# Layer 1's product scan keeps its last value in a 449th column of shifted PSUM banks, and one copy of twelve columns per band replaces twelve copies of one

## The reference

```
x_dbl = einsum('kd,bdl->bkl', x_proj_w, xs)
dts, Bs, Cs = (x_dbl[:, :R], x_dbl[:, R:R + N], x_dbl[:, R + N:])
delta = softplus(einsum('dr,brl->bdl', dt_w, dts) + dt_b)
log_dA = maximum(delta * A, LOG_EPS)
P = exp(cumsum(log_dA))
dB_u = delta * Bs * xs
hs = P * cumsum(dB_u / maximum(P, EPS))
y = einsum('bdnl,bnl->bdl', hs, Cs) + xs * Ds
```

## Time and profile before

| | us |
|---|---|
| median of three runs | 4020.88 |
| lowest and highest | 4011.57, 4022.5 |
| the profiled execution, its own time | 4020.36 |
| its span | 4018.6 |
| mean granted TensorE clock, share of full | 0.928 |
| start of the first product scan (group 0) | 1956.5 |
| start of the last group | 3765.1 |

### The profile page before, as it was taken

The page is one execution under the profiler, slowest core; times in us unless marked ns, Lnnn a source line. Parts: engine busy times, 40 slices in busy tenths (PEclk is TensorE's granted clock), DMA queues, the critical chain, the costliest instruction groups (busy, mean ns, idle before and its releaser), DMA issues. The chain is left out here.

```text
span 4018.6 us, 72697 instructions
## 1 busy us (share of the span) xinstructions
PE 3650.8 (91%) x22358; PEld 2646.6 (66%) x22358; DVE 3106.0 (77%) x4416; ACT 2571.1 (64%) x4292; POOL 2575.8 (64%) x2672
## 2 busy tenths in 40 slices
PE   6999999999999999997899998998989989899776
PEld 6888787979787887877565564664646646466322
DVE  3675758475756667570499998999989989989999
ACT  1463728172735546274688787787778878777754
POOL 0352717162634536270488888888979889888988
PEclk9999999999999999998799898998989989989877
DMA  7546473747465554428565564655546646465222
GB/s 225 170 138 204 104 250 95 251 102 234 109 200 149 164 181 125 149 76 181 130 177 143 162 170 124 172 152 147 164 127 181 169 125 173 129 168 158 86 75 60
DMA packets 383746, 612.84 MB, mean 153 GB/s; under 512 B 199967, under 2 KB 324152, under 8 KB 383048
## 3 DMA queue, kind: packets, MB, share of 16 engines
q1 hardware_dynamic: 383336, 607.74, 53.5%
HBM read 527.35 MB, written 80.28 MB: 151 GB/s over the span
## 5 line engine op out<-in xcount | busy, mean ns | idle before, releaser
L321 POOL TENSOR_TENSOR h_low<-act_h,h_high 128x448 fp32r<-128x448 f32 x448 | 598.0, 1354 | 724.1 <-ACT h_high L520 723.9
L515 ACT ACTIVATE act_h<-ps_up,b 128x448 f32<-128x448 f32 x672 | 408.7, 635 | 728.5 <-PE ps_up L633 728.2
L1348 PE MATMUL ps_y<-h,ident 128*128 128x448 f32 x1344 | 727.1, 629 | 144.3 <-POOL h L1036 113.1
L1036 POOL TENSOR_TENSOR h<-h,c_rows 128x448 f32<-128x448 f32 x672 | 763.7, 1136 | 51.2 <-DVE h L1126 5.7
L1023 POOL TENSOR_TENSOR u<-dxs,b_rows 128x448 f32<-128x448 f32 x672 | 764.5, 1138 | 27.9 <-DVE ps_q L1115 16.8
L1099 DVE TENSOR_TENSOR_SCAN ps_q<-d_a,q_last,ps_q 128x448 f32<-128x448 f32 x576 | 659.5, 1145 | 0.0
L1126 DVE TENSOR_TENSOR_SCAN h<-d_a,h_last,ps_q 128x448 f32<-128x448 f32 x576 | 645.3, 1120 | 0.0
L1300 PEld LDWEIGHTS ps_front<-win,taps 120*112 120x112 f32 x4608 | 540.5, 188 | 149.2 <-issue 147.2
L606 PE MATMUL ps_stage<-win,taps 124*112 124x112 f32 x6144 | 608.3, 261 | 2.7 <-DVE w_low L368 2.7
L606 PEld LDWEIGHTS ps_stage<-win,taps 124*112 124x112 f32 x6144 | 608.1, 178 | 3.2 <-DVE w_low L368 2.8
L1205 ACT ACTIVATE d_a<-delta,log_eps,a_neg 128x448 f32<-128x448 f32 x672 | 503.3, 750 | 114.0 <-DVE h L1126 58.5
(11 more groups left out here) (81 smaller groups left out, 6212.6 us busy)
## 6 DMA issues: line engine op xcount, KB each, us to landing
taps<-in_t_dram SPq DMA_DIRECT2D x192, 896.0 KB, 5.0
taps<-in_t_dram SPq DMA_DIRECT2D x192, 672.0 KB, 4.7
b_rows<-bc_dram SPq DMA_DIRECT2D x224, 224.0 KB, 3.0
c_rows<-bc_dram SPq DMA_DIRECT2D x224, 224.0 KB, 3.1
xres<-in_x_dram SPq DMA_DIRECT2D x224, 168.0 KB, 2.5
x_dram<-x1o SPq DMA_DIRECT2D x224, 168.0 KB, 2.0
x1pad<-x_dram SPq DMA_DIRECT2D x96, 392.0 KB, 6.0
out_dram<-y SPq DMA_DIRECT2D x168, 224.0 KB, 2.6
```

The costliest lines, as they stand in the source:

```text
L321: nc.gpsimd.tensor_tensor(h_low[u % 2][:, t, :], act_h[u % 2][:, t, :], h_high[u % 2][:, t, :], ALU.subtract).then_inc(h_low_ready[t], 1)
L515: nc.scalar.activation(act_h[u % 2][:, t, :], ps_up[t][:, 0:BT], ACT.Gelu, bias=b1[:, t:t + 1]).then_inc(gelu_done, 1)
L1036: nc.gpsimd.tensor_tensor(h[s % H_SLOTS][:, :], h[s % H_SLOTS][:, :], c_rows[n][:, :], ALU.mult).then_inc(hc_done, 1)
L1348: nc.tensor.matmul(total, ident[:, :], h[s % H_SLOTS][:, :], start=False, stop=(n == N - 1)).then_inc(y_added, 1)
```

## The change

- `ps_q` becomes one tensor of two banks of 512 columns. A step of number j in its band uses bank j % 2 and starts in column 5 - j // 2, so that each use of a bank begins one column lower than the last one.
- The product scan runs over 449 columns. Column 448 of every d_a buffer is set to 1.0 once, by seven GpSimd memsets at the layer's start, and ScalarE writes only the first 448. The 449th value of the scan is then the last value of q once more; it lies one column beyond what the next step in that bank writes, and so stays.
- After the twelfth step's scan, one copy takes the six kept columns of both banks (128x12) into `q_last`; twelve copies of one column are gone. The gates no longer wait for `q_kept`; only the first product scan of a band does.

```diff
-        d_a = [sb(f"d_a{i}", [128, BT]) for i in range(DA_SLOTS)]
+        d_a = [sb(f"d_a{i}", [128, BT + 1]) for i in range(DA_SLOTS)]
-        ps_q = [pb(f"ps_q{i}") for i in range(2)]
+        ps_q = ctx.enter_context(nc.psum_tensor("ps_q", [128, 2, BANK], F32))
-        no_q = ps_q[0][:, BT:BT + 1]
+        no_q = ps_q[:, 0, BANK - 1:BANK]
+        PAIRS = STEPS // 2
+        def q_start(s):
+            return PAIRS - 1 - s % STEPS // 2
+        def q_bank(s, cols=BT):
+            return ps_q[:, s % 2, q_start(s):q_start(s) + cols]
+        def q_carry(s):
+            k = s % 2 * PAIRS + q_start(s)
+            return q_last[:, k:k + 1]
+            for k in range(DA_SLOTS):
+                nc.gpsimd.memset(d_a[k][:, BT:BT + 1], 1.0).then_inc(prepared, 1)
 def scan_q(g, s):
-                if s > 1:
-                    dve.wait_ge(q_kept, g * KEPT + min(s - 1, KEPT))
-                first = q_first[:, 0:1] if b == 0 else q_last[:, j:j + 1]
-                nc.vector.tensor_tensor_scan(ps_q[s % 2][:, 0:BT], d_a[s % DA_SLOTS][:, :],
-                                             no_q.broadcast_to([128, BT]), first,
+                if b > 0 and j == 0:
+                    dve.wait_ge(q_kept, g * (BANDS - 1) + b)
+                nc.vector.tensor_tensor_scan(q_bank(s, BT + 1), d_a[s % DA_SLOTS][:, :],
+                                             no_q.broadcast_to([128, BT + 1]), q_first[:, 0:1] if b == 0 else q_carry(s),
                                              ALU.mult, ALU.add).then_inc(q_done, 1)
-            def keep_q(g, s):
-                b, j = s // STEPS, s % STEPS
-                if b + 1 < BANDS:
-                    dve.wait_ge(q_done, g * S + s + 1)
-                    nc.vector.tensor_copy(q_last[:, j:j + 1], ps_q[s % 2][:, BT - 1:BT]).then_inc(q_kept, 1)
+            def keep_q(g, b):
+                dve.wait_ge(q_done, g * S + (b + 1) * STEPS)
+                nc.vector.tensor_copy(q_last[:, :].rearrange("p (k j) -> p k j", k=2),
+                                      ps_q[:, :, BT:BT + PAIRS]).then_inc(q_kept, 1)
 def gate(g, s):
-                if b + 1 < BANDS:
-                    dve.wait_ge(q_kept, g * KEPT + s + 1)
 def group(g, more):
-                    keep_q(g, s)
+                    if j == STEPS - 1 and b + 1 < BANDS:
+                        keep_q(g, b)
```

More of the change, by code:

```diff
@@ L800, in layer1 @@
         BORDERS = 4
-        PREPARED = 4 + TILES + 1
+        PREPARED = 4 + TILES + 1 + DA_SLOTS
         S = BANDS * STEPS
@@ L1095, in scan_q @@
                 dve.wait_ge(h_done, g * S + max(s, 1))
-                if s > 1:
-                    dve.wait_ge(q_kept, g * KEPT + min(s - 1, KEPT))
-                first = q_first[:, 0:1] if b == 0 else q_last[:, j:j + 1]
-                nc.vector.tensor_tensor_scan(ps_q[s % 2][:, 0:BT], d_a[s % DA_SLOTS][:, :],
-                                             no_q.broadcast_to([128, BT]), first,
-                                             ALU.mult, ALU.add).then_inc(q_done, 1)
-            def keep_q(g, s):
-                b, j = s // STEPS, s % STEPS
-                if b + 1 < BANDS:
-                    dve.wait_ge(q_done, g * S + s + 1)
-                    nc.vector.tensor_copy(q_last[:, j:j + 1], ps_q[s % 2][:, BT - 1:BT]).then_inc(q_kept, 1)
+                if b > 0 and j == 0:
+                    dve.wait_ge(q_kept, g * (BANDS - 1) + b)
+                nc.vector.tensor_tensor_scan(q_bank(s, BT + 1), d_a[s % DA_SLOTS][:, :],
+                                             no_q.broadcast_to([128, BT + 1]), q_first[:, 0:1] if b == 0 else q_carry(s),
+                                             ALU.mult, ALU.add).then_inc(q_done, 1)
+            def keep_q(g, b):
+                dve.wait_ge(q_done, g * S + (b + 1) * STEPS)
+                nc.vector.tensor_copy(q_last[:, :].rearrange("p (k j) -> p k j", k=2),
+                                      ps_q[:, :, BT:BT + PAIRS]).then_inc(q_kept, 1)
             def gate(g, s):
-                b = s // STEPS
                 dve.wait_ge(q_done, g * S + s + 1)
-                if b + 1 < BANDS:
-                    dve.wait_ge(q_kept, g * KEPT + s + 1)
                 dve.wait_ge(u_done, g * S + s + 1)
-                nc.vector.scalar_tensor_tensor(ps_q[s % 2][:, 0:BT], ps_q[s % 2][:, 0:BT], 1.0, u[s % U_SLOTS][:, :],
+                nc.vector.scalar_tensor_tensor(q_bank(s), q_bank(s), 1.0, u[s % U_SLOTS][:, :],
                                                ALU.min, ALU.mult).then_inc(gated, 1)
@@ L1125, in scan_h @@
                     first = h_last[:, j:j + 1]
-                nc.vector.tensor_tensor_scan(h[s % H_SLOTS][:, :], d_a[s % DA_SLOTS][:, :], ps_q[s % 2][:, 0:BT], first,
+                nc.vector.tensor_tensor_scan(h[s % H_SLOTS][:, :], d_a[s % DA_SLOTS][:, 0:BT], q_bank(s), first,
                                              ALU.mult, ALU.add).then_inc(h_done, 1)
@@ L1204, in clip_a @@
                     act.wait_ge(h_done, g * S + s - DA_SLOTS + 2)
-                nc.scalar.activation(d_a[s % DA_SLOTS][:, :], delta[:, t, :], ACT.Relu, bias=log_eps[:, 0:1],
+                nc.scalar.activation(d_a[s % DA_SLOTS][:, 0:BT], delta[:, t, :], ACT.Relu, bias=log_eps[:, 0:1],
                                      scale=a_neg[:, t, n:n + 1]).then_inc(clipped, 1)
@@ L1210, in exp_a @@
                 act.wait_ge(clipped, g * S + s + 1)
-                nc.scalar.activation(d_a[s % DA_SLOTS][:, :], d_a[s % DA_SLOTS][:, :], ACT.Exp,
+                nc.scalar.activation(d_a[s % DA_SLOTS][:, 0:BT], d_a[s % DA_SLOTS][:, 0:BT], ACT.Exp,
                                      bias=LOG_EPS).then_inc(d_a_ready, 1)
```

## The result

The changed kernel took 3986.5 us, the median of six runs (3978.3 to 4003.1), beside 4021.7 us for the kernel before: a ratio of 0.9916, with a 95% interval of 0.9890 to 0.9941. In a later comparison (run 11) it took 3972.7 us against 4029.2, a ratio of 0.9858 (0.9836 to 0.9880). Forecast were 3960 us, 61 less; it gained 35 and 57 us. The first gain is nearly rival B's 31 us, the second nearly the forecast's.

What follows compares the result with a forecast made beforehand. VectorE was taken to set undisturbed bands, with other engines close behind. Looped groups 45.5 us plus last group 15.5 us gave 61 us off 4020.4, rounded to 3960 us; own range 3940 to 3978, stated range 3925 to 3998.

Steps and rivals of the forecast that it cites:

- rival B: Looped groups: TensorE's chain holds them, waits move to before sum_delta; 31 us gained, 3989 us (3975 to 4005); chance 0.22.
- What bounds the kernel now: Layer 1: VectorE, busy 34.78 of 35.20 us, sets the length of an undisturbed band; other engines close behind.
- What a copy costs: VectorE's steps, bands 0 to 5: 0.19 us per copy in looped groups, 0.25 in the last; 114 us in all.
- What is added: VectorE: 48 wide copies at 0.2 us, 10 us; 449th column 1.6 us; register work ahead of scan_h nothing.
- Looped groups, bands 1 to 4: These four bands together fall from 143.1 to 137 us per looped group: 6 us gained, TensorE limiting the rest.
- ScalarE's earlier handover: Bands 1 to 4: ScalarE, paced by VectorE, comes earlier, so TensorE's waits go and its clock stays up; part of 6 us.
- Bands 0, 5 and 6: Looped groups: band 0 gains 0.5 us behind its last wait, band 5 is taken as 0, band 6 has no copies: nothing.
- The last group: No front there, only GpSimd's 32.9 us near; six bands fall from 35.9 to 33.3 us, 15.5 us gained.
- A: VectorE keeps its whole gain, TensorE's idling vanishing and clock staying up: 99 us gained, 3921 us; chance 0.13.
- C: GpSimd's products grow longer by alignment, as buffers behind d_a start 28 bytes later: slower, 4060 us; chance 0.03.
- D: VectorE gives the saving back through register work ahead of scan_h or a slower shifted-bank scan: 4010 us; chance 0.04.

Runs made afterwards that it cites:

- run 11: The changed kernel unchanged, timed again with a second trace: 3972.7 us against 4029.2 for the kernel before, ratio 0.9858.
- run 2: Kernel before the change, with a third of layer 1's convolution matmuls left out: 4000.0 us, ratio 0.9933.
- run 8: Kernel before the change, with each of its 576 one-column copies made twice: 4052.2 us, ratio 1.0066.
- run 7: Changed kernel plus an idle one-column copy in each of the eleven other steps of bands 0 to 5, awaited by no gate: step 2.68 us; timed later, 3978.5 us.
- run 1: Kernel before the change, with all 576 one-column copies and their waits left out (no carry of q): 3972.5 us, ratio 0.9875.
- run 3: Changed kernel with a third of layer 1's convolution matmuls left out: 3930.5 us, ratio 0.9764.

## Why the prediction was right, and where not

- **What bounds the kernel now** held. Runs 2 and 8 show VectorE setting bands 2 and 4 of the kernel before, and the 35.2 us under which bands 1 and 3 could not fall; in those two TensorE's chain added up to 1.5 and 1.0 us.
- **What a copy costs**: 0.19 and 0.25 us a step, 114 us in all, were right as a sum: steps fell to 2.61 us. As a price of the instruction they were not. It was read off a step that also held the gate's wait; the copy's own share is 0.07 us (run 7). Of the Trainium skill, "VectorE: DVE Perf Modes", the estimate of 126 ns from the errata section's cycles fits the copy's duration of 0.13 us but not what it costs, 0.07. The DRAIN section says that a semaphore costs nothing extra; that does not hold for this copy, where waiting for one (with the register work beside it) costs 0.12 us.
- **What is added**: 0.2 us for a wide copy was three times too much; the gate follows it after 0.06 us, and does not wait for it. The 449th column and the register work cost nothing that shows (run 1: 0.1 us a band for all of it).
- **Looped groups, bands 1 to 4**: predicted 6 us gained and 137 us left; gained 5.0 (34.8 over seven), with 136.9 left in group 2. The step that ScalarE's earlier handover lets TensorE's waits and its lower clock shrink also showed: TensorE's waits for ScalarE's window copies fell from 4.0 to 1.7 us, and band 4's clock rose from 0.90 to 1.00. Where the gain would lie was not foreseen: bands 2 to 4 were to be 33.5 to 35 us each, and came to 33.0, 35.9 and 33.0. Bands 2 and 4 took VectorE's whole 2.2 us each, band 3 next to nothing.
- **Bands 0, 5 and 6**: this is the step that failed. Forecast were 0.5, 0 and 0 us gained; in the trace they lost 10.7 + 2.7 + 5.5 = 18.9 us over seven groups. I had put band 0 down to the wait for C rows, and treated its length as given. In every looped band 0 of both traces TensorE is busy for all but 5.1 to 7.0 us, most of which is one pause; so the band is as long as that pause and TensorE's work at the clock that it is granted, 37.7 to 43.4 us before (the earlier trace rows are from a group with 43.2) and 39.0 to 46.0 after. Two traces of the changed kernel differ by 9 us in it. Why the clock falls more in one group than in the next is open, and so it is open whether the change made band 0 longer at all. In band 6 GpSimd is busy 36.10 of 36.40 us before and 36.80 of 37.10 after (group 2): having waited for C rows in band 5 it catches up here, and in the trace after half of the chain of work that ended last runs through its products in that band. Why it has 0.7 us more there is open too.
- **The last group**: 15.5 predicted, 17.4 measured; GpSimd lags without VectorE waiting for it.
- **The rivals**: A was 99 us and needed TensorE to give way; even with a third of the convolution gone the change was worth 69.5 (runs 2 and 3). B had its number in the first measurement, and its waits in bands 1 and 3, up to 2.8 us; in bands 2 and 4 VectorE waits for nothing. C: GpSimd's products stayed at 1136 ns. D: the undisturbed step is 2.61 us.

So the mechanism of the gain was the predicted one. The size was off by the term for bands 0, 5 and 6, mis-sized by 0.5 + 18.9 / 7 = 3.2 us per looped group, 22 us in all, of which 9 are gone in the second trace of the same kernel; bands 1 to 4 gave 7 us less than forecast, the last group 2 more. The first measurement, 3986.5 us, is outside the forecast's own 3940 to 3978 us and inside the stated range only because that takes in most of B; the second, 3972.7, is inside both. Between their traces 9 of the 11 us are band 0, whose length the prediction took as given, and to that extent the closeness of the second is luck.

## What to carry to other kernels

The wait for a small instruction can cost more than the instruction: here 0.12 to 0.19 us for the wait and 0.07 us for the copy. Look at the distance between starts with and without it, and first take away the wait, then the instruction. When an engine that is busy 99% of a stretch is made faster, add up the next engine's work band by band; of bands 1 to 4 the gain was there in full in the two where TensorE then shows 32.1 us busy, and not in the two with 35.0 and 34.2. And before a part of a program is booked as "not changed", look whether it has more than one length in the trace of before; if it goes with the granted clock, it can come out otherwise in the next trace, with or without an edit.

## What the runs showed of the hardware that I had not expected

- A busy TensorE is no protection for its clock. In 2747 to 2770 us of the changed kernel it is busy without a gap, with matmuls and transposes of 32 partitions in turns, and is granted 0.55:

```profile
2747.00:2770.00 23.00, 23.00 (x97) 12.40 (x97) 11.54 (x14) 16.38 (x28) 17.58 (x22) 0.55 0.59 169
```

- More work made it faster: four further matmuls of 128x448 per group cut the time at 1.2 GHz in band 0 from between 19 and 41 us to between 8 and 14 us, and the kernel's ratio from 0.9858 at best to 0.9809. With nine such matmuls in band 6 instead (run 5) it was 14 to 36 us in the bands 0 behind them.
- The PSUM copy of one column delays the next instruction by 0.05 us when nothing waits for it and by 0.17 us, in the last group 0.22 us, when the next one does.
